# A mixture-of-experts layer whose gathers add expert results straight into the residual in SBUF

## The chip, the cores and the metric

The kernel runs on one core of a Trainium2 chip, in one launch. The metric is the device time of that launch in microseconds: the median of repeated runs.

## What is computed

The reference takes x of shape (16, 512, 128) in float32 and adds four sublayers to it, each on the layernorm of the running x: an attention without softmax (causal scores, 16 heads of 8 columns), a mixture of experts, an attention that keeps only its 6 strongest queries per head, and the same mixture of experts again. What matters here is the mixture:

```python
logits = xf @ router_w; probs = softmax(logits)       # 8192 tokens, 16 experts
w, idx = top_k(probs, 2)                               # two experts each
keep = rank_within_expert < capacity; w = where(keep, w, 0)
xe = x_pad[dispatch]                                   # rows sorted by expert
hidden = silu(xe @ gate_w[e]) * (xe @ up_w[e])
out = (hidden @ down_w[e]) * wbuf                      # scaled by its weight
combined.at[dispatch].add(out);  x = x + combined
```

## The kernel before

The tokens are 64 tiles of 128 tokens, 4 tiles to a batch, 16 batches. The residual x stays in SBUF all the time (`xs`, 128 x 64 x 128). The work goes through these stages, with all instruction streams written out by hand and tied by semaphores:

- First attention (`attention_a`, 16 batches). Beside it, a few batches behind, the router picks two experts for each token, and GpSimd (POOL) sends the normed rows to DRAM.
- First mixture, `experts(0)` and `experts(1)`: batches 0 to 7, then 8 to 15. Each has GRP = 24 groups of 512 rows.
- Second attention (`body`, called by `each_four`, 16 batches). For each batch b, the results of the first mixture for batch b+2 are fetched and added while the scores of b run.
- Second mixture, `experts(2)` and `experts(3)`, again 24 groups each; in `experts(3)` the fetching for batches 0 to 7 runs beside the groups. Then what is left of the fetching, and the output.

How rows move. `places` (L513) works out, on POOL, where each of a token's K = 2 copies goes, and the product of the router's weight and `keep`, which it leaves in `wts` in SBUF (L531). `send` (L498) issues 8 indirect scatters for a batch, tile by tile and both copies of a tile together: 128 rows of 512 bytes each from `xnf` to `dispA` or `dispB` in DRAM. `xnf` is a ring of NF = 3 buffers, and the norm of batch n waits until the sends of n-3 have landed. Before a mixture starts, its area's tails, and once the whole of `dispB`, are filled with zeros from `zeros`.

In `experts`, SyncE (SP) loads the rows of group g+4 (L387, two DMAs of 128 KB) when TensorE has turned group g (`xe_tp`), and then stores the results of group g-2 (L416). For each group TensorE turns the rows (`turn_x`, L1812), multiplies with the gate and up weights (L1823) and with the down weights of the group before (L1834); ScalarE evicts `xeT` (L845) and takes the silu (L850), VectorE (DVE) makes the hidden product (`hidden`, L1293), copies the result from PSUM to `ye` (`y_copy`, L1301), and then runs `pieces`, its share of other work. The order on DVE is hidden(g), y_copy(g-1), pieces(g).

Results come back by `fetch` (L557): for each batch, 8 indirect gathers on POOL, 128 rows each, from `ybufA` or `ybufB` into a buffer `yg` (shared with `vmyg`). `indices` on DVE copies the row numbers first (L1313), and a fetch waits for them. Then DVE adds each tile twice, xs = yg * wts + xs (L1318), eight instructions a batch: in groups 5 to 11 of `experts(1)` for the first two batches; in the scores of pairs 18 to 21 of each batch of the second attention; in groups 5 to 21 of `experts(3)`, where the indices of batch b+2 are made after the adds of batch b (`add_all`); and after it. The last batch is added in two parts (L1604), so that its first three tiles go out while the fourth is fetched. SP's `out` stores (L444 to L448) wait for the adds.

`stored(seg)` on POOL holds back the first fetch of a mixture half until all its results are in DRAM.

Of the kernel before, what the change touches and what calls it, by code (L numbers as in the profile page):

```python
# [5 lines left out]
F32 = mybir.dt.float32  # L6
# [7 lines left out]
P = 128  # L14
# [41 lines left out]
NF = 3  # L56


def build(nc, w, out):
    ctx = ExitStack()  # L60
    with ctx:
# [6 lines left out]
        def sem(name):  # L68
# [3 lines left out]
        dispA = nc.dram_tensor("dispA", [DUMMY + UR, D], F32).ap()  # L72
        dispB = nc.dram_tensor("dispB", [DUMMY + UR, D], F32).ap()
# [9 lines left out]
        wts = sb("wts", [P, NT * K])  # L83
# [21 lines left out]
        zeros = sb("zeros", [P, UT * D])  # L105
# [28 lines left out]
        xnf = [sb(f"xnf{r}", [P, TB, D]) for r in range(NF)]  # L134
# [22 lines left out]
        slg = [sb(f"slg{h}", [P, TB * K], I32) for h in range(2)]  # L157
        vmyg = sb("vmyg", [P, TB * GH * (D + DH)])
        vm = vmyg[:, :].rearrange("p (t x) -> p t x", t=TB)
        yg = [vmyg[:, h * TB * K * D:(h + 1) * TB * K * D].rearrange("p (j d) -> p j d", d=D) for h in range(2)]  # L160
# [29 lines left out]
        tails = sb("tails", [1, E], I32)  # L190

        apart = [sb(f"apart{h}", [P, GH, SEQ]) for h in range(2)]
        whose = sb("whose", [P, NT * K, E])
        xe = [[apart[h][:, r, :].rearrange("p (j d) -> p j d", d=D) for r in range(NX)] for h in range(2)]
# [43 lines left out]
                 "slg_ready got0 got1 got_end comb_head combined_head comb0 combined "  # L238
# [91 lines left out]
        def _(sp):  # L330
# [43 lines left out]
            for e in range(E):  # L374
# [3 lines left out]
                             zeros[:, :].unsqueeze(1).to_broadcast([P, SPAN // UR, UT * D])).then_inc(s["zeroed"], 16)  # L378
# [32 lines left out]
            def experts(seg):  # L411
# [29 lines left out]
            experts(3)  # L441
            for i in range(B - 1):
                sp.wait_ge(s["combined"], i + 1 + B)
                sp.dma_start(out_b[i], xs[:, tiles_of(i), :]).then_inc(s["x_out"], 16)  # L444
            sp.wait_ge(s["combined_head"], 1)
            sp.dma_start(out_b[B - 1][:, 0:TB - 1, :], xs[:, NT - TB:NT - 1, :]).then_inc(s["x_out"], 16)
            sp.wait_ge(s["combined"], 2 * B)
# [5 lines left out]
        def _(pool):  # L453
# [10 lines left out]
            pool.memset(vmyg[:, :], 0.0).then_inc(s["vm_zero"], 1)  # L464
# [33 lines left out]
            def send(g, i, h, tiles=range(TB)):  # L498

                if 0 in tiles:  # L500
                    pool.wait_ge(s["slots_ready"], g + 1)
# [1617 lines left out]
```

## Time and profile before

| | us |
|---|---|
| median of 3 runs | 1412.83 (1411.5 to 1418.56) |
| span of the profiled execution | 1555.5 |
| TensorE busy in the span | 1331.6 |
| VectorE busy | 1056.7 |
| GpSimd busy | 833.1 |
| ScalarE busy | 759.3 |

The profiled execution has no time of its own on record other than its span of 1555.5 us, from the first to the last instruction; it is 10% above the median of the runs without the profiler. All durations below are of that execution. The page gives the busy time of each engine, the span in slices, the DMA queues, the chain of work that ended last, and the costliest groups of instructions; the trace behind it can be asked for a stretch of time, an engine or a line.

### The profile page before, as it was taken

The page shows a single profiled execution, that of the slowest core. Times are in us where ns is not written, and L with a number is a line of the kernel's source. Part 1 is how long each engine was busy: PE and PEld are TensorE (multiplying, and loading weights), DVE is VectorE, ACT ScalarE, POOL GpSimd, SP SyncE. Part 2 cuts the span into 40 slices and gives each one's busy share as a digit, 9 for nine tenths or more (in the row PEclk, how much of TensorE's full clock was granted, in tenths as well). Part 3 has the DMA queues.
Part 4 walks back from the last instruction along what each step waited for, and adds up shares of the span by engine and source line. Part 5 has one row for each costly group of instructions (what it writes and reads, how often), then busy time and mean ns, then how long its engine had stood idle before and what let it go on. Part 6 is the DMA issues. An engine that isn't in the chain of part 4 may idle for free.

```text
span 1555.5 us, 28624 instructions
## 1 busy us (share of the span) xinstructions
PE 1331.6 (86%) x8534; PEld 822.4 (53%) x8534; DVE 1056.7 (68%) x4590; ACT 759.3 (49%) x1901; POOL 833.1 (54%) x1246
## 2 busy tenths in 40 slices
PE   3999998978996989999999999999999999767400
PEld 1566655547885955444444444444455588656400
DVE  2899998883643477888778788787798546433422
ACT  2444444424544666666556566555566455333200
POOL 3247776675323133466666567755555345435576
PEclk9999998987998988999889799887699899988755
DMA  6755312013444410000000000020001134444432
GB/s 171 244 171 188 115 38 69 25 52 111 157 151 135 137 31 15 15 21 28 25 25 28 18 25 28 27 77 23 23 18 42 34 122 153 132 129 138 145 79 73
DMA packets 119785, 125.82 MB, mean 81 GB/s; under 512 B 15568, under 2 KB 109904, under 8 KB 119632
## 3 DMA queue, kind: packets, MB, share of 16 engines
q1 hardware_dynamic: 103248, 90.42, 18.3%
q0 software_dynamic: 16384, 33.59, 7.5%
q8 instruction: 68, 1.11, 0.3%
q14 instruction: 85, 0.70, 0.2%
HBM read 50.15 MB, written 73.79 MB: 80 GB/s over the span
## 4 chain that ended last, share of the span: by engine, by line
PE 68%; DVE 9%; issue 6%; another core or an unknown queue 5%; POOL 5%; ACT 4%; DMA 0%; ACTq 0%; POOLq 0%; DVEq 0%
PE pair L1897 27%; PE pair L1823 8%; PE pair L1834 4%; POOL vmyg L563 4%; PE pair L1685 4%; PE bank L1709 3%; DVE pT L1126 2%; PE pair L1812 2%; PE bank L1630 2%; DVE pT L1401 2%; PE bank L1925 1%; PE bank L1624 1%; PE bank L1951 1%; PE pair L1674 1%
## 5 line engine op out<-in xcount | busy, mean ns | idle before, releaser
L1897 PE MATMUL pair<-kT,apart 32*128 32x512 f32 x2048 | 500.4, 733 | 8.0 <-DVE smax L1401 6.5
L1401 DVE CUSTOM_DVE_ANT_0 pT<-pair,pT 128x256 f32<-128x256 f32 x1024 | 385.4, 417 | 128.5 <-ACT pT L924 110.1
L924 ACT ACTIVATE pT<-pair 128x256 f32<-128x256 f32 x1024 | 327.1, 395 | 257.1 <-PE pair L1897 229.2
L1897 PEld LDWEIGHTS pair<-kT,apart 32*128 32x128 f32 x2048 | 198.5, 208 | 155.4 <-DVE smax L1401 97.8
L563 POOL DMA_INDIRECT vmyg<-ybufA,slg x128 | 123.2, 962 | 149.8 <-DVE smax L1401 67.3
L1293 DVE TENSOR_TENSOR hid<-sg,pair 128x512 f32<-128x512 f32 x96 | 65.9, 686 | 197.6 <-ACT sg L850 171.2
L1823 PE MATMUL pair<-xeT,unit_w 128*128 128x256 f32 x768 | 195.6, 400 | 0.8 <-issue 0.8
L563 POOL DMA_INDIRECT vmyg<-ybufB,slg x128 | 122.7, 958 | 91.9 <-DVE smax L1401 47.6
L1126 DVE TENSOR_TENSOR pT<-pair,causal 128x512 f32<-128x512 f32 x256 | 159.5, 681 | 12.5 <-PE pair L1685 12.3
L1834 PE MATMUL pair<-unit_w,hid 128*128 128x128 f32 x768 | 110.7, 291 | 61.9 <-DVE ye L1301 61.6
L508 POOL DMA_INDIRECT dispB<-xnf,sli x128 | 127.4, 996 | 63.7 <-issue 36.2
L1823 PEld LDWEIGHTS pair<-xeT,unit_w 128*128 128x128 f32 x768 | 149.0, 205 | 19.6 <-issue 1.2
L508 POOL DMA_INDIRECT dispA<-xnf,sli x128 | 128.3, 1002 | 56.5 <-issue 35.8
L1834 PEld LDWEIGHTS pair<-unit_w,hid 128*128 128x128 f32 x768 | 106.6, 204 | 72.6 <-DVE hid L1293 34.8
L1318 DVE SCALAR_TENSOR_TENSOR xs<-vmyg,wts,xs 128x128 f32<-128x128 f32 x248 | 80.1, 376 | 57.7 <-DMA vmyg<-ybufB,slg 54.6
L850 ACT ACTIVATE sg<-pair 128x512 f32<-128x512 f32 x96 | 57.3, 597 | 110.9 <-PE pair L1823 67.9
L857 ACT ACTIVATE unit_w<-f_w 128x384 f32 x160 | 74.9, 516 | 42.6 <-PE pair L1834 27.0
L1301 DVE COPY ye<-pair 128x512 f32<-128x512 f32 x96 | 65.8, 685 | 30.4 <-remote 17.8
L1401 DVE DVE_READ_ACCUMULATOR2_ANT smax<- 128x1 f32 x1024 | 83.1, 81 | 0.0
L550 POOL TENSOR_SCALAR lnv<-mv 128x4 f32<-128x4 f32 (+1 forms) x51 | 12.0, 235 | 132.8 <-DVE mv L1023 125.6
L845 ACT ACTIVATE xeT<-pair 128x512 f32<-128x512 f32 x96 | 56.3, 586 | 54.1 <-remote 26.6
L1685 PE MATMUL pair<-apart,kT 32*128 32x512 f32 x512 | 76.2, 665 | 7.6 <-DVE pT L1126 7.3
(231 smaller groups left out, 2008.0 us busy)
## 6 DMA issues: line engine op xcount, KB each, us to landing
dispB<-zeros SPq DMA_DIRECT2D x16, 1408.0 KB
apart<-dispA SPq DMA_DIRECT2D x96, 128.0 KB
ybufA<-ye SPq DMA_DIRECT2D x48, 256.0 KB
apart<-dispB SPq DMA_DIRECT2D x96, 128.0 KB
ybufB<-ye SPq DMA_DIRECT2D x48, 256.0 KB
dispA<-zeros SPq DMA_DIRECT2D x33, 128.0 KB
xs<-in_x SPq DMA_DIRECT2D x16, 256.0 KB, 3.2
out<-xs SPq DMA_DIRECT2D x15, 256.0 KB
```

What stands on the lines that cost most here:

```text
L508: pool.indirect_dma_start(out=area, out_offset=bass.IndirectOffsetOnAxis(ap=sli[h][:, K * j + k:K * j + k + 1], axis=0), in_=xnf[g % NF][: ...
L563: pool.indirect_dma_start(out=yg[h][:, j, :], out_offset=None, in_=ybuf[second(g)], in_offset=bass.IndirectOffsetOnAxis(ap=slg[h][:, j:j + ...
L857: last = act.activation(unit_w[g % NX][:, u, :], f_w[:, bass.ds(ex[u], 1), :].rearrange("p a n -> p (a n)"), ACT.Copy)
L924: act.activation(rel[n % RING][:, q, :], pair[n % RING][:, q, HALF:SEQ], ACT.Relu).then_inc(s["relu_done"], 1)
L1126: dve.tensor_tensor(pT[n % (2 * NG)][:, :, :], bank[4 + n % 4].rearrange("p (j t) -> p j t", j=GH), causal[:, :].unsqueeze(1).to_broadcast ...
L1293: dve.tensor_tensor(hid[h][:, :, :].rearrange("p j n -> p (j n)"), sg[h][:, :, :].rearrange("p j n -> p (j n)"), bank[4 + 2 * h][:, :], AL ...
L1318: last = dve.scalar_tensor_tensor(out=xb, in0=yg[h][:, K * j + k, :], scalar=wts[:, bass.ds((b * TB + j) * K + k, 1)], in1=xb, op0=ALU.mul ...
L1401: dve.tensor_tensor_reduce(out=rel[n % RING][:, q, :], in0=pair[n % RING][:, q, 0:HALF], in1=rel[n % RING][:, q, :], scale=1.0, scalar=LOW ...
L1685: pe.matmul(bank[4 + g][:, :].rearrange("p (j t) -> p j t", j=GH), kTs[h][at, c * P:(c + 1) * P], apart[h][at, :, c * P:(c + 1) * P], star ...
L1823: last = pe.matmul(bank[3 + 2 * h + k][:, u * UR:(u + 1) * UR], unit_w[r][:, u, k * D:(k + 1) * D], xeT[h][:, UT * u:UT * (u + 1), :].rear ...
L1834: last = pe.matmul(bank[7][:, j * D:(j + 1) * D], hid[h][:, j, :], unit_w[r][:, j // UT, 2 * D:3 * D], start=True, stop=True)
L1897: pe.matmul(pair[n % RING][:, q, :], apart[h][at, j, t * P:(t + 1) * P], kTs[h][at, HALF:], start=True, stop=True).then_inc(s["bsc_done"], 1)
```

## The change

The row of the dispatch area gets a 129th element, the token's weight for that expert. `xnf`, `zeros`, `dispA`, `dispB` and the `xe` buffers are widened from D = 128 to R = 129 elements. `places` writes the weight of the first choice into column 128 of `xnf` and keeps that of the second in `wsecond`. `send` no longer goes by tiles but by choices: first the four tiles with the first choice; then it waits until they have landed, POOL copies the second weight into the column, and the four tiles go out again. In `experts`, DVE copies the 4 weights of a group out of the loaded rows (`weights`, before `hidden`), and `y_copy` becomes a multiplication of PSUM by these weights. SP now stores group g-2 before it loads group g+4, and that load waits for `weights(g)` instead of the transposes. `fetch` gathers with the DMA's own addition straight into `xs`, four tiles of the first choice and four of the second, and the second choice waits for the first to have landed. The buffers `yg`, `slg` and `wts`, the index copies, and all additions on DVE are gone. In the tail the order is: batch b's first choice, then batch b-1's second.

```diff
+R = D + 1
-        dispA = nc.dram_tensor("dispA", [DUMMY + UR, D], F32).ap()
+        dispA = nc.dram_tensor("dispA", [DUMMY + UR, R], F32).ap()
...
             def load(seg, g):
                 if g >= NX:
-                    sp.wait_ge(s["xe_tp"], seg * GRP + g - NX + 1)
+                    sp.wait_ge(s["wrow_done"], seg * GRP + g - NX + 1)
...
                 for g in range(GRP - 1):
+                    if g >= 2:
+                        store(g - 2)
                     if g + NX < GRP:
                         load(seg, g + NX)
-                    if g >= 2:
-                        store(g - 2)
...
+            def send(g, i, h, parts=range(TB)):
                 area = disp[second(g)]
+                for part in parts:
+                    k = part // 2
+                    if part == 0:
+                        pool.wait_ge(s["slots_ready"], g + 1)
+                        pool.wait_ge(s["xw_done"], g + 1)
...
+                    if part == 2:
+                        pool.wait_ge(s[f"sent{h}"], 16 * TB * (K * i + 1))
+                        pool.tensor_copy(xnf[g % NF][:, :, D:R], wsecond[h][:, :, :]).then_inc(s["second_done"], 1)
+                        pool.wait_ge(s["second_done"], g + 1)
+                    for j in (part % 2 * 2, part % 2 * 2 + 1):
                         pool.indirect_dma_start(
...
-                pool.tensor_tensor(wts[:, cols].rearrange("p (t k) -> p t k", k=K), topw[:, :, :], keep[:, :, :], ALU.mult)
+                pool.tensor_tensor(wsecond[h][:, :, :], topw[:, :, 1:2], keep[:, :, 1:2], ALU.mult)
+                pool.tensor_tensor(xnf[g % NF][:, :, D:R], topw[:, :, 0:1], keep[:, :, 0:1], ALU.mult).then_inc(s["xw_done"], 1)
...
+            def fetch(b, g, k, tiles=range(TB), end=()):
+                h = g % 2
+                if 0 in tiles:
+                    pool.wait_ge(s["slots_made"], g // HALFB + 1)
+                    if g >= 2:
+                        pool.wait_ge(s[f"got{k}{h}"], g // 2 * 16 * TB)
+                    if k:
+                        pool.wait_ge(s[f"got0{h}"], (g // 2 + 1) * 16 * TB)
+                for t in tiles:
+                    at = (b * TB + t) * K + k
                     pool.indirect_dma_start(
-                        out=yg[h][:, j, :], out_offset=None, in_=ybuf[second(g)],
-                        in_offset=bass.IndirectOffsetOnAxis(ap=slg[h][:, j:j + 1], axis=0),
-                    ).then_inc(s["got_end" if j in end else f"got{h}"], 16)
+                        out=xs[:, b * TB + t, :], out_offset=None, in_=ybuf[second(g)],
+                        in_offset=bass.IndirectOffsetOnAxis(ap=slots[:, at:at + 1], axis=0), compute_op=ALU.add,
+                    ).then_inc(s["got_end" if t in end else f"got{k}{h}"], 16)
...
+                def weights(g):
+                    dve.wait_ge(s["xe_tp"], g + 1 + base)
+                    dve.tensor_copy(wrow[g % NX][:, :].unsqueeze(2), xe[seg % 2][g % NX][:, :, D:R]).then_inc(s["wrow_done"], 1)
...
-                    dve.tensor_copy(ye[h][:, :, :].rearrange("p j d -> p (j d)"), bank[7][:, :]).then_inc(s["y_ready"], 1)
+                    dve.tensor_tensor(ye[h][:, :, :], bank[7][:, :].rearrange("p (j d) -> p j d", d=D),
+                                      wrow[g % NX][:, :].unsqueeze(2).to_broadcast([P, GT, D]), ALU.mult).then_inc(s["y_ready"], 1)
...
-            def add_choice(b, h, k, done, tiles=range(TB)):
-                for j in tiles:
-                    last = dve.scalar_tensor_tensor(out=xb, in0=yg[h][:, K * j + k, :],
...
-                        add_first(b + 2, h, ((0, 1), (2, 3))[n - 18])
-                        add_second(b + 2, h, ((0, 1), (2, 3))[n - 20])
```

## Rows read from the trace of the kernel before

**Rows 1.** Busy time of each engine by stage (windows in us), as columns name.
```profile
core 0: us, PE busy (x) PEld busy (x) DVE busy (x) ACT busy (x) POOL busy (x), PEclk, DMA share, GB/s
352.00:461.00 109.00, 98.23 (x617) 88.98 (x618) 54.02 (x158) 55.91 (x106) 41.40 (x72) 0.90 0.44 140
461.00:549.00 88.00, 70.96 (x447) 64.05 (x447) 35.74 (x77) 45.28 (x90) 21.29 (x27) 0.92 0.44 136
549.00:1228.00 679.00, 668.98 (x3032) 323.23 (x3032) 544.29 (x2942) 413.34 (x1223) 395.02 (x544) 0.87 0.09 26
1228.00:1345.00 117.00, 101.56 (x614) 87.58 (x607) 60.65 (x217) 59.95 (x116) 46.51 (x76) 0.93 0.38 120
1345.00:1466.00 121.00, 85.11 (x465) 75.31 (x463) 48.61 (x109) 43.95 (x86) 59.74 (x63) 0.86 0.44 131
1466.00:1555.50 89.50, 0.00 (x0) 0.00 (x0) 23.77 (x89) 0.00 (x0) 62.43 (x66) 0.51 0.37 99
```

**Rows 2.** Timeline of POOL, gathers in experts(3) and behind it.
```profile
1348.26 1.01 POOL L563 DMA_INDIRECT vmyg<-ybufA,slg  x1 [4.51 <-DMA ybufA<-ye]
...
1469.32 0.94 POOL L563 DMA_INDIRECT vmyg<-ybufB,slg  x1 [1.28 <-issue]
...
1550.08 0.94 POOL L563 DMA_INDIRECT vmyg<-ybufB,slg  x1 [0.30 <-issue]
```

**Rows 3.** Waits: who waited for whom, us in total, times, longest.
```profile
POOL vmyg L563 <- DVE slg L1313: 48.6, 7, 13.3
```

**Rows 4.** SP timeline, then chain of waits, in clean groups of experts(1).
```profile
496.68 0.85 SPq L387 DMA_DIRECT2D apart<-dispB  x2
...
497.04 0.44 PE pair L1812 x4
497.48 1.73 PE pair L1823 x8
499.21 0.89 PE pair L1834 x8
```

**Rows 5.** Timeline of DVE, the last two adds of the kernel.
```profile
1552.73 0.74 DVE L1604 SCALAR_TENSOR_TENSOR xs<-vmyg,wts,xs 128x128 f32<-128x128 f32 x2 [0.84 <-DMA vmyg<-ybufB,slg]
```

**Rows 6.** Timeline of DVE in the second attention: a batch with adds, one without.
```profile
949.98 0.69 DVE L1439 TENSOR_REDUCE amax<-bank 128x1 f32<-128x512 f32 x1
961.95 0.27 DVE L1447 TENSOR_TENSOR cxm<-bank,block 128x128 f32<-128x128 f32 x1
...
1173.55 0.69 DVE L1439 TENSOR_REDUCE amax<-bank 128x1 f32<-128x512 f32 x1
1185.58 0.27 DVE L1447 TENSOR_TENSOR cxm<-bank,block 128x128 f32<-128x128 f32 x1
```

**Rows 7.** Timeline of DVE, two neighbouring groups of experts(1), adds between them.
```profile
491.31 0.68 DVE L1301 COPY ye<-pair 128x512 f32<-128x512 f32 x1
491.91 1.13 DVE L1318 SCALAR_TENSOR_TENSOR xs<-vmyg,wts,xs 128x128 f32<-128x128 f32 x4
...
494.37 0.68 DVE L1301 COPY ye<-pair 128x512 f32<-128x512 f32 x1
```

**Rows 8.** Groups of instructions: busy us, mean ns of one, idle before.
```profile
L508 POOL DMA_INDIRECT dispA<-xnf,sli x128 | 128.3, 1002 | 56.5 <-issue 35.8 <-DVE xs L1140 12.4 <-DVE pT L1126 4.9
L563 POOL DMA_INDIRECT vmyg<-ybufB,slg x128 | 122.7, 958 | 91.9 <-DVE smax L1401 47.6 <-issue 35.7 <-DVE slg L1313 8.6
L1293 DVE TENSOR_TENSOR hid<-sg,pair 128x512 f32<-128x512 f32 x96 | 65.9, 686 | 197.6 <-ACT sg L850 171.2 <-issue 24.9 <-DVE slots L1276 0.7
```

**Rows 9.** DMA queue of POOL: packets, MB, share of 16 engines.
```profile
q0 software_dynamic: 16384, 33.59, 7.5%
```

**Rows 10.** The last send of experts(2) (POOL), loads of experts(3) (SP), a scatter's landing (chain).
```profile
1323.56 0.97 POOL L508 DMA_INDIRECT dispB<-xnf,sli  x1 [0.30 <-issue]
1336.67 2.97 SPq L387 DMA_DIRECT2D apart<-dispB  x4
...
193.78 4.10 DMA dispA<-xnf,sli
```

More of the change, by code:

```diff
@@ L133, in build @@
         xnT = sb("xnT", [P, SEQ])
-        xnf = [sb(f"xnf{r}", [P, TB, D]) for r in range(NF)]
+        xnf = [sb(f"xnf{r}", [P, TB, R]) for r in range(NF)]
         xfT = sb("xfT", [P, SEQ])
@@ L156, in build @@
         sli = [sb(f"sli{h}", [P, TB * K], I32) for h in range(2)]
[L157 to L160, printed above, removed]
+        vm = sb("vm", [P, TB, GH * (D + DH)])
         cnt = sb("cnt", [P, K, E])
@@ L190, in build @@
         tails = sb("tails", [1, E], I32)
-        apart = [sb(f"apart{h}", [P, GH, SEQ]) for h in range(2)]
+        wsecond = [sb(f"wsecond{h}", [P, TB, 1]) for h in range(2)]
+        wrow = [sb(f"wrow{r}", [P, GT]) for r in range(NX)]
+        apart = [sb(f"apart{h}", [P, GH, GT * R]) for h in range(2)]
         whose = sb("whose", [P, NT * K, E])
-        xe = [[apart[h][:, r, :].rearrange("p (j d) -> p j d", d=D) for r in range(NX)] for h in range(2)]
+        xe = [[apart[h][:, r, :].rearrange("p (j d) -> p j d", d=R) for r in range(NX)] for h in range(2)]
         xeT = [sb(f"xeT{h}", [P, GT, D]) for h in range(2)]
@@ L656, in _ @@
             stored(0)
-            fetch(0, 0)
-            fetch(1, 1)
+            for k in range(K):
+                for b in range(2):
+                    fetch(b, b, k)
             def selected_rows(b):
@@ L754, in _ @@
             stored(2)
-            fetch(B, 0)
-            fetch(B + 1, 1)
-            for b in range(2, B):
+            for b in range(B):
                 if b == HALFB:
+                    fetch(b - 1, B + b - 1, 1)
                     stored(3)
-                fetch(B + b, b % 2, end=range(K * (TB - 1), K * TB) if b == B - 1 else ())
+                fetch(b, B + b, 0)
+                if b % HALFB:
+                    fetch(b - 1, B + b - 1, 1)
+            fetch(B - 1, 2 * B - 1, 1, end=(TB - 1,))
         @block.scalar
@@ L804, in keys_turns @@
                 for j in range(GH):
-                    last = act.activation(apart[h][:, j, :], qTs[h][:, :], ACT.Copy, scale=inturn[:, j:j + 1])
+                    last = act.activation(apart[h][:, j, 0:SEQ], qTs[h][:, :], ACT.Copy, scale=inturn[:, j:j + 1])
                 last.then_inc(s["turns_ready"], 1)
@@ L886, in masked_q @@
                 for j in turns:
[L887 removed]
+                    last = act.activation(apart[k][:, j, 0:SEQ], bank[0][:, :], ACT.Identity, bias=qbias[:, j:j + 1],
                                           scale=inturn[:, j:j + 1])
@@ L1466, in body @@
                         residual(b - 2)
-                    if fetch and n == 1:
-                        indices(b + 2, h)
                     if b == MID + 2 and n == 29:
```

123 lines of the change are left out of this document (31 added, 92 removed).

## The prediction

> **What bounds the kernel now.** I read the stages first [rows 1]. The reader is to see three kinds. In the second attention (679 us) TensorE is busy for 669; in the four halves of the mixture (109 + 88 + 117 + 121 = 435 us) no engine is full; in the last 89.5 us TensorE does nothing and POOL is busy for 62.4. That last stretch is a queue of gathers [rows 2]: the first gather of the second half starts at 1469.32, the 64th at 1550.08, 1.28 us apart on the average and 1.25 as a rule (0.94 of work, 0.30 between two). POOL issues them without a gap and nothing else decides. Ahead of it stand the 64 gathers of the first half, from 1348.26 on. They should take 64 x 1.25 = 80 us, but take 120, because POOL waited for index copies that DVE makes behind its adds: 48.6 us in 7 waits [rows 3], 8.6 of which lie in the second attention [rows 8] and 40.0 here. The gathers of the second half may start only when `experts(3)` has stored its last result, and the two came together: after 1469.32 less a wait of 1.28 [rows 2]. So in the profile the end of the kernel is: end of `experts(3)`, plus 64 gathers.
>
> Then the clean pace of a group [rows 4]: 0.44 for the transposes, 1.73 for gate and up, 0.89 for down, 3.06 us, all on TensorE. 96 groups at it are 294 us, and the four halves took 435: 141 us are stalls. The span of 1555.5 stands 142.7 above the median of 1412.83. That the two are so alike suggests that the timed runs have few of these stalls; it is an inference, and no row shows an execution without the profiler. It matters for the sum: undisturbed, `experts(3)` takes 24 x 3.06 = 73 us, less than the 80 us of its 64 gathers, so that in a timed run POOL's 128 gathers (160 us) follow each other from the end of `experts(2)` to the end of the kernel, in both kernels. I make the sum for the profiled execution and then say what the other picture changes.
>
> **What goes, with what it is worth.** (a) The 112 adds of the second attention, 8 a batch, and 14 index copies. A batch with adds and one without can be compared, both at the full clock (the granted level 2.4 GHz): from the reduction of `amax` to `cxm`, pairs 18 to 26, it is 949.98 to 961.95 = 11.97 us with the 8 adds and 4 statistics, and 1173.55 to 1185.58 = 12.03 without any of them [rows 6]. So these adds cost nothing: TensorE sets that stretch. The index copy stands where DVE is dense, at pair 1, at most 0.1 us a batch: 0 to -1.4 us; I take -1. (b) The adds of `experts(1)`: with four adds (1.13 us) between them two result copies are 3.06 apart [rows 7], the clean pace: 0. (c) The adds and index copies of `experts(3)`: 40 us of POOL's waits go, but the gathers they delay weren't late, since the end of the half came at the same time; in the undisturbed picture only the first of these waits stays, some 1.5 us (the index copy after group 6, at 7 x 3.06 = 21.4 us, against 20 us for 16 gathers). I take -1. (d) At the very end the two last adds, 0.74 us, and the step to them [rows 5]: -0.8.
>
> **What comes, and what hides it.** (e) `y_copy` as a multiplication reads PSUM and SBUF like `hidden`, which takes 686 ns [rows 8] where the copy took 0.68 [rows 7]: 0. The 96 weight copies of 4 numbers are 0.1 to 0.2 us each; DVE has room for 1.13 us more in a group at the clean pace [rows 7]: 0, and 96 x 0.15 = 14 us if that room were gone. (f) The load of group g+4 now waits for `weights(g)`, which stands behind y_copy(g-2) on DVE; so it goes out about one group (3.06 us) later than now. A load at 496.68 [rows 4] is for a group three clean groups on, some 9 to 10 us, of which 6 to 7 stay. The nearest row of a landing is 4.10 us, of a scatter [rows 10]: hidden, 0, and up to 1 us a group where the landing is over 7. (g) `send`: between the fourth and the fifth scatter POOL waits for landing, up to 4.10 less the 0.97 of issue, and copies a column (0.2). Beside the attentions these two are in different slots, tens of TensorE steps apart: 0. In a mixture they are back to back: +3.3 us for each of 3 batches. Behind the waiting POOL stands the next `places`, and for the last batch SP waits for its sends before it loads the first rows of the next half. Its last send starts at 1323.56, and SP loads at 1336.67 [rows 10]: 9 us of slack here after landing; at the clean pace the load would be due four groups after the sends began, about when they land. So 0 to 3.3 us at each of two places; I take +2 in all. (h) Rows of 516 bytes instead of 512 in the scatters, the loads and the zero fill, no longer at multiples of 512. No row shows such a transfer; DMA shares of 0.38 to 0.44 in the mixture [rows 1] leave room for a quarter more: 0, bounds 0 and +3. (i) The fetch of a second choice waits for the first. In the tail, four gathers of another batch (5.0 us) lie in between, which covers a landing of 4.10 with 0.9 to spare: 0. In the second attention POOL waits 1 to 3 us a batch, and it works 395 us of 679 [rows 1]: 0.
>
> (j) The price of a gather that adds. This decides, and no row shows one. The lower end is that of a gather now: 0.94 and 0.30. Nothing excludes less, but no reason speaks for it. For the upper end I take half as much again, as for three addresses a row (source, old value, target) instead of two: +0.47, which is 64 x 0.47 = 30 us behind `experts(3)`, and 128 x 0.47 = 60 if POOL has no gap in the timed runs. The nearest row between is the scatter, which differs from a gather in its direction and a bounds check: 1002 against 958 ns in the mean [rows 8], +0.04. One more operand should cost more than another direction, and less than half of everything, as a part of the 0.94 is fixed; I take +0.08, nearer to the scatter. In the profile's picture 64 x 0.08 = +5, in the undisturbed one 128 x 0.08 = +10. The transfers themselves stay hidden: the queue of POOL held 7.5% of 16 engines' 1555.5 us [rows 9], so each of 512 gathers and scatters took 0.075 x 1555.5 / 512 = 0.23 us of each engine; doubled, that is 0.46 in a cadence of 1.25.
>
> What the row shows here is a cost of issue, 0.94 us on POOL. The Trainium skill (Collectives: The Full Stack, the section on the bandwidth ceiling) says of an addition in the DMA engines that the add itself is free but needs two source reads, with two read descriptors on the same ring, and that such a transfer ran at about half the rate of a copy. By that rule the engines' 0.23 us would become up to 0.46, and the time would not change, since the issue sets the pace. If the second read descriptor also doubled POOL's whole work, the same 128 gathers would cost 128 x 0.94 = 120 us more; no row bears that out, and it is not in my sum. The skill's page DMA: Bandwidth & Descriptors calls the generation of descriptors a small, variable part of a DMA's fixed cost; by it, the surcharge would be near nothing.
>
> The sum: -1 -1 -0.8 +2 = -0.8 without the surcharge, and +10 for it in the picture that I hold likelier for timed runs: 1412.8 - 0.8 + 10 = 1422 us. In the profile's picture it is 1412.8 - 0.8 + 5 = 1417.
>
> **The rivals.** *No surcharge.* The adding gather is issued like any other. For it: 128 rows are few, and a scatter costs almost the same [rows 8]. Time: 1412.8 - 0.8 = 1412, between 1409 and 1415.
>
> *A dear gather.* From +0.25 to +0.47 on each, 128 times: +32 to +60, 1444 to 1472. For it: 0.94 us for 128 rows may well be work by the row. Against it: only that scatter and gather are so alike. The same side has a smaller case: if an adding gather lands later than the 5.0 us that lie between the two choices, each of 16 second fetches of the tail waits; at 7 us that is 16 x 2 = 32, 1444.
>
> *Faster.* `experts(3)` ends earlier, as its stalls are of the gathers' making. At the clean pace its 24 groups take 73 us, in the profile 121, 5.04 a group [rows 1]. In the changed kernel the first 64 gathers run without POOL's waits and are over by 1348 + 80 = 1428; the remaining 38 us to 1466 then hold 12 clean groups instead of 7.5, five groups less to do later: 5 x 3.06 = -15 us in the profile. It decides from the point where the stalls exist in timed runs and the surcharge is under 0.1 us: 1398 to 1405. Against it: the stalls are there in `experts(2)` too, which took 117 us with no gather beside it [rows 1]. One rule leads the same way: the Trainium skill (SBUF — State Buffer, the section on who interferes with whom) says that a DVE instruction with two inputs in SBUF, which an add is, holds back a GpSimd instruction that reads SBUF. The gathers beside adds and those without are equally long here, 0.94 [rows 2], so that I give it nothing.
>
> **How the numbers follow.** The forecast, a surcharge of 0.03 to 0.25, has 0.42: 1416 to 1444, with the likeliest at 1422. No surcharge 0.25. A dear gather 0.15, a late landing 0.05. Faster 0.13. For this kernel about 0.5%, 7 us, can be told from no change: 1405.8 to 1419.9. Faster by more: 0.13. Within: 0.25 and the 0.10 of the forecast that lies under 1420, 0.35. Slower: 0.32 + 0.15 + 0.05 = 0.52. The range from 1401 to 1450 leaves out half of the faster case and two thirds of the dear one, 0.17.
>
> **What would show it.** Right: the gathers of the tail on POOL have one length of 0.97 to 1.2 us, 0.30 apart, and still no gap; DVE loses some 34 us of busy time in the second attention (112 adds of 0.30) while that stage keeps its 679 us; the groups of `experts(1)` stay 3.06 apart; two columns' copies on POOL stand behind a wait of some 3 us in `experts(0)` and `experts(2)`. Wrong: gathers of 0.94 (then 1412); waits on the landing of the first choice in the tail; a TensorE that waits for loaded rows every group; or an `experts(3)` well under 121 us, which would make it faster.

## The result, and the profile after

The changed kernel takes 1562.85 us (median of 4 runs, 1556.42 to 1566.97) against 1412.38 beside it: 1.109 times as long [1.104, 1.114], 150 us more. The forecast was 1422, and the range ended at 1450.

The page of the changed kernel, parts 1 and 3:

```profile
span 1563.4 us, 28579 instructions
PE 1311.2 (84%) x8534; PEld 819.3 (52%) x8534; DVE 988.9 (63%) x4398; ACT 755.7 (48%) x1901; POOL 999.3 (64%) x1310
q0 software_dynamic: 45056, 33.72, 12.6%
```

VectorE has lost work, and POOL has 166 us more than in the first profile. The queue of POOL moves almost the same bytes as in [rows 9] (the scattered rows now have 516 bytes), in 45056 packets instead of 16384.

One thing has to be put right first. The profile of the kernel before stood 142.7 us above its median. The same kernel profiled again has a span of 1400.8 us, and it is this trace (`before_again`) that the changed one is laid beside. By stage (first mixture, second attention, second mixture, rest), the kernel before and then the changed one:

```profile
354.00:507.00 153.00, 149.54 (x979) 137.15 (x977) 86.88 (x228) 97.09 (x189) 58.14 (x84) 1.00 0.55 172
507.00:1143.00 636.00, 625.87 (x3098) 317.71 (x3099) 548.84 (x2993) 417.97 (x1237) 399.99 (x547) 0.95 0.10 30
1143.00:1302.00 159.00, 153.86 (x1016) 140.86 (x1014) 99.63 (x274) 97.14 (x188) 96.09 (x126) 1.00 0.58 177
1302.00:1401.00 99.00, 1.64 (x13) 1.29 (x11) 25.77 (x91) 0.25 (x1) 70.15 (x75) 0.52 0.36 100
```

```profile
360.00:515.00 155.00, 148.92 (x974) 136.70 (x972) 87.58 (x257) 96.85 (x189) 70.42 (x90) 1.00 0.60 170
515.00:1229.00 714.00, 692.19 (x3094) 348.96 (x3095) 516.60 (x2868) 417.36 (x1237) 470.64 (x573) 0.84 0.14 27
1229.00:1391.00 162.00, 157.28 (x1024) 144.10 (x1021) 92.40 (x266) 97.59 (x188) 102.06 (x115) 0.98 0.63 170
1391.00:1563.00 172.00, 1.20 (x9) 0.97 (x8) 1.83 (x3) 0.00 (x0) 140.94 (x92) 0.52 0.39 63
```

The columns are those of [rows 1]. The mixtures take almost the same. Two stages have grown: the end by 73 us, and the second attention by 78, in which TensorE's granted clock fell from 0.95 to 0.84. The end is the gathers; first, 65th and last of the second mixture on POOL, before and after:

```profile
1233.43 1.01 POOL L563 DMA_INDIRECT vmyg<-ybufA,slg  x1 [4.29 <-DMA ybufA<-ye]
1314.97 0.94 POOL L563 DMA_INDIRECT vmyg<-ybufB,slg  x1 [0.30 <-issue]
1395.59 0.94 POOL L563 DMA_INDIRECT vmyg<-ybufB,slg  x1 [0.30 <-issue]
```

```profile
1322.02 2.46 POOL L580 DMA_INDIRECT xs<-ybufA,slots  x1 [6.77 <-issue]
1441.43 1.55 POOL L580 DMA_INDIRECT xs<-ybufB,slots  x1 [0.30 <-issue]
1558.10 1.55 POOL L580 DMA_INDIRECT xs<-ybufB,slots  x1 [0.30 <-issue]
```

In both, 128 gathers follow each other from the end of `experts(2)` to the end of the kernel, 162.2 and 236.1 us from the start of the first to the start of the last. The work of one is 1.55 us instead of 0.94 [rows 2], the gap between two still 0.30: a surcharge of 0.60 us. (128 surcharges are 77 us, and the tail has grown by 74: in the 162.2 stand a gather of 1.99 us and a gap of 2.13, which `plain` below, with 158.6 us, doesn't have.)

Here is how the other stage loses time. TensorE in one batch of it, changed kernel (start, us, engine, line), and TensorE's windows around the place (columns as above, the clock third from the end):

```profile
793.51 1.13 PE L1855 MATMUL pair<-kT,apart 32*128 32x512 f32 x4
797.41 1.08 PE L1582 MATMUL bank<-ident,xnf 128*128 128x128 f32 x4 [2.77 <-POOL xnf L698]
798.42 2.08 PE L1855 MATMUL pair<-kT,apart 32*128 32x512 f32 x4
```

```profile
788.00:792.00 4.00, 4.00 (x19) 1.32 (x20) 3.43 (x17) 2.46 (x9) 3.63 (x3) 1.00 0.27 33
792.00:796.00 4.00, 2.64 (x16) 0.88 (x10) 3.13 (x19) 3.31 (x10) 3.68 (x6) 0.99 0.14 16
796.00:800.00 4.00, 2.59 (x8) 1.22 (x8) 0.32 (x2) 0.60 (x1) 3.42 (x5) 0.50 0.05 17
...
812.00:816.00 4.00, 4.00 (x14) 1.56 (x13) 3.18 (x25) 1.43 (x6) 1.34 (x2) 0.50 0.09 29
816.00:820.00 4.00, 3.92 (x24) 2.48 (x23) 3.15 (x15) 2.52 (x9) 0.93 (x2) 0.95 0.08 25
```

TensorE stands for 2.77 us, since POOL hasn't finished the normed rows `xnf` that the router needs. Behind it the granted clock is 0.50 (the 1.2 GHz level) for some 20 us, although TensorE is busy without a break again from 797.41 on, and the same four score matmuls take 2.08 us instead of 1.13. In the kernel before, `xnf` is ready (838.43 + 1.04, a row shown further down) about 4.1 us before TensorE asks:

```profile
843.62 0.66 PE L1624 MATMUL bank<-ident,xnf 128*128 128x128 f32 x4
```

The stage windows say how much of the loss is clock. What the granted share falls short of full is 0.05 x 636 = 32 us in the kernel before and 0.16 x 714 = 114 us in the changed one: 82 us more, where the stage grew by 78, and TensorE is busy for 692 of its 714 us. So nearly all of this stage's loss is time that TensorE worked at the lower level; the waits themselves are short.

### The profile page after: what moved, and what is told of

Read it like the earlier page. It is cut to its first block and busy times, and to the rows that moved or that the text cites. A ratio compares the mean times of both kernels' runs of the same rounds, so it can differ in the third digit from the quotient of the medians.

```text
span 1563.4 us, 28579 instructions
## 1 busy us (share of the span) xinstructions
PE 1311.2 (84%) x8534; PEld 819.3 (52%) x8534; DVE 988.9 (63%) x4398; ACT 755.7 (48%) x1901; POOL 999.3 (64%) x1310
## 3 DMA queue, kind: packets, MB, share of 16 engines
q0 software_dynamic: 45056, 33.72, 12.6%
## 5 line engine op out<-in xcount | busy, mean ns | idle before, releaser
L580 POOL DMA_INDIRECT xs<-ybufA,slots x128 | 200.1, 1563 | 110.7 <-DVE smax L1403 67.5
L580 POOL DMA_INDIRECT xs<-ybufB,slots x128 | 199.8, 1561 | 85.9 <-DVE smax L1403 51.4
L1781 PE MATMUL pair<-xeT,unit_w 128*128 128x256 f32 x768 | 185.4, 385 | 0.0
L1146 DVE TENSOR_TENSOR pT<-pair,causal 128x512 f32<-128x512 f32 x256 | 159.5, 681 | 14.8 <-PE pair L1643 14.5
L1781 PEld LDWEIGHTS pair<-xeT,unit_w 128*128 128x128 f32 x768 | 141.2, 194 | 15.4
L1792 PE MATMUL pair<-unit_w,hid 128*128 128x128 f32 x768 | 101.9, 276 | 8.9 <-DVE ye L1327 8.9
L1792 PEld LDWEIGHTS pair<-unit_w,hid 128*128 128x128 f32 x768 | 100.1, 192 | 15.7 <-DVE hid L1313 10.7
L1327 DVE TENSOR_TENSOR ye<-pair,wrow 128x512 f32<-128x512 f32 x96 | 65.7, 684 | 11.4 <-issue 7.3
L1667 PE MATMUL bank<-pT,vm 128*32 128x128 f32 x2048 | 71.5, 282 | 0.0
L1770 PE MATMUL pair<-ident,apart 128*128 128x128 f32 x384 | 60.6, 282 | 6.0 <-ACT xeT L865 3.2
```

The lines of the kernel that those rows point to most:

```text
L580: pool.indirect_dma_start(out=xs[:, b * TB + t, :], out_offset=None, in_=ybuf[second(g)], in_offset=bass.IndirectOffsetOnAxis(ap=slots[:, ...
L1146: dve.tensor_tensor(pT[n % (2 * NG)][:, :, :], bank[4 + n % 4].rearrange("p (j t) -> p j t", j=GH), causal[:, :].unsqueeze(1).to_broadcast ...
L1667: last = pe.matmul(bank[1][at:at + QG, c * P:(c + 1) * P], vm[:, c, j * P + at:j * P + at + QG], pT[c % 2 * NG + g][:, j, :], start=(c == ...
L1781: last = pe.matmul(bank[3 + 2 * h + k][:, u * UR:(u + 1) * UR], unit_w[r][:, u, k * D:(k + 1) * D], xeT[h][:, UT * u:UT * (u + 1), :].rear ...
L1792: last = pe.matmul(bank[7][:, j * D:(j + 1) * D], hid[h][:, j, :], unit_w[r][:, j // UT, 2 * D:3 * D], start=True, stop=True)
```

## The experiments

Where gathers don't add, they replace the rows of the residual, which is lost; such kernels serve for their time alone. Beside the kernels, the one before ran at 1407.51, 1408.08, 1406.64, 1409.2 and 1402.9 in the five groups of runs.

**Which profile is typical.** `before_again`: the kernel before, unchanged.

> The kernel before, once more with a profile, to see whether the span of its first profile (1555.5 us, against a median of 1412.8) belongs to every profiled execution. If the 141 us of stalls in the mixture halves belong to that one execution, this profile has a span near 1413, the four halves last about 4 x 74 to 80 = 300 us, and POOL's 128 gathers follow each other from the end of experts(2) to the end. If they belong to the profiler, the span is again near 1555 and the halves near 435 us.

1402.55 us, span 1400.8. The 48 groups of each mixture last 153 and 159 us, 312 where the first profile had 435: most of the stalls belonged to the first profile's execution, and the "undisturbed picture" of the prediction is the right one.

**The addition or the rest.** `plain` has no `compute_op`; the edit of `add_first` is below, and `add_second` has `g >= B` in its place:

```diff
                         in_offset=bass.IndirectOffsetOnAxis(ap=slots[:, at:at + 1], axis=0),
-                        compute_op=ALU.add,
+                        **({"compute_op": ALU.add} if g < B else {}),
```

> The changed kernel with the DMA's addition left out of all gathers: a gathered row replaces the one in xs, so that the residual is lost. All else stays: carried weights, scaled results, split sends, order of loads and stores. Theory A (the addition in the gathers makes the whole loss, in the tail and in the second attention): gathers of 0.94 us, 0.30 apart, and a time within 10 us of before, 1405 to 1422. Theory B (the addition costs only its surcharge of 0.60 on the 128 gathers of the tail, 77 us, and the other edits make the remaining 73): 1486, from 1475 to 1497.

> The changed kernel with the DMA's addition only in the gathers of the first mixture (beside the second attention); those of the second mixture replace the residual. Theory A: 1563 - 128 x 0.60 = 1486, since the tail is freed of its surcharge, and the loss of 73 in the second attention stays. Theory B: 1486 too, as the 73 belong to the other edits. The second attention lasts about 715 us, and the tail about 160 for 128 gathers. This run checks the 77; the two theories are told apart by the next one.

> The changed kernel with the DMA's addition only in the gathers of the second mixture; those of the first replace the residual. Theory A (adding gathers cost 73 in the second attention): 1413 + 77 = 1490, from 1480 to 1500, and a second attention near 640 to 650 us. Theory B (they cost nothing there): 1563, from 1555 to 1570, and a second attention near 715.

`plain` 1404.53, 0.9985 [0.995, 1.002] of the kernel before; `add_first` 1491.37 (1.058); `add_second` 1480.15 (1.052). Theory A holds. Carried weights, scaled results, split sends, wider rows, the order of loads and stores, and all of VectorE's additions are together worth nothing. The additions cost 76 us in the second mixture and 87 in the first; the sum, 162, is close to the 158 between `plain` and the changed kernel. In `add_second` the second attention has its old length, and the tail shows the surcharge alone:

```profile
1245.20 1.64 POOL L580 DMA_INDIRECT xs<-ybufA,slots  x1 [7.01 <-issue]
1363.89 1.55 POOL L580 DMA_INDIRECT xs<-ybufB,slots  x1 [0.30 <-issue]
1480.61 1.55 POOL L580 DMA_INDIRECT xs<-ybufB,slots  x1 [0.31 <-issue]
```

**Is it the addition by itself?** `before_adding`: the kernel before, with the addition in its gathers (on top of what stands in `yg`).

```diff
-                        in_offset=bass.IndirectOffsetOnAxis(ap=slg[h][:, j:j + 1], axis=0),
+                        in_offset=bass.IndirectOffsetOnAxis(ap=slg[h][:, j:j + 1], axis=0), compute_op=ALU.add,
```

> The kernel before with the DMA's addition in its gathers (into yg, on top of what stands there) and nothing else changed; DVE still adds. If the addition in the gathers is the whole loss, whatever else is changed: 1407 + 77 + 75 = 1559 (1540 to 1575), gathers of 1.55 us. If it needs the other edits (the wait of a second choice for the first, the split sends): at most 1407 + 77 = 1484 with a second attention of 640.

1507.11 (1.071). Neither of the two forecasts: the tail is 74 us longer as it should be, but the second attention lasts 663 us, not 715. So the surcharge costs some 25 us there in the old order, and the change brings something that triples it.

**Lateness or transfers?** `half` (only second choices add), `ahead` (the fetches earlier in the batch), `late_plain` and `late_more` (nothing adds, but POOL has extra copies to make).

```diff
                 if fetch_:
-                    pair_made(1)
-                    fetch(b + 2, b + 2, 0, (0, 1))
+                    fetch(b + 2, b + 2, 0)
                 if b >= 3:
                     places(b - 3, b - 3 + B, 1 - h)
...
+                    fetch(b + 2, b + 2, 1)
```

```diff
                     ).then_inc(s["got_end" if t in end else f"got{k}{h}"], 16)
+                    if g < B:
...
+                        pool.tensor_copy(linger[n % 4][:, :], zeros[:, 0:240]).then_inc(s["lingered"], 1)
```

> The changed kernel with the DMA's addition only in the gathers of the second choices; those of the first choices replace the residual. POOL is then late by 4 x 0.60 = 2.4 us a batch instead of 4.8. Theory A (a threshold: in the kernel before the normed rows are ready at 839.5 where TensorE asks for them at 843.6, so that up to 4.1 us of lateness cost nothing): second attention 637 to 645 us, the tail 64 x 0.60 = 38 us longer, 1405 + 38 = 1443 (1435 to 1452). Theory B (every adding gather costs its share, wherever it stands): 1405 + (75 + 77) / 2 = 1481, second attention near 678.

> The changed kernel, complete, with the gathers of the second attention issued earlier in each batch: all four of the first choice before places, all four of the second right behind it, without their waits for score pairs. Theory A (the dearer gathers make POOL late with the normed rows xnf; TensorE waits for them 1 to 3 us a batch, and its granted clock falls to 0.50 for some 16 to 20 us afterwards; together 75 us): the norm is done 4 to 5 us earlier, TensorE no longer waits for it, the second attention lasts 637 to 645 us, and the time is 1563 - 75 = 1488 (1478 to 1498). Theory B (the adding transfers themselves disturb the attention, whenever they are issued, or POOL's work as a whole is the bound): the second attention stays above 700 and the time at 1555 to 1570.

> The kernel `plain` (gathers replace the residual, none adds), with one more copy on POOL (128 x 240 elements, some 0.6 us by the nearest row, 0.73 for 128 x 256) behind each gather of the second attention, so that POOL is as late as with adding gathers but no DMA adds. Theory A (POOL's time alone makes the loss): the second attention lasts 700 to 730 us and the time is 1405 + 75 = 1480 (1460 to 1495), with TensorE waiting for xnf. Theory B (the adding transfers make it): second attention 640, time 1405 (1400 to 1415).

> As late_plain, but two copies of 0.39 us behind each gather of the second attention instead of one, since in late_plain the spacing of the gathers rose only from 1.25 to 1.53 us. Still no gather adds. The spacing should be 1.9 us here, as with adding gathers (1.85), and POOL 8 x 0.65 = 5.2 us late a batch. Theory A (POOL's time alone makes the loss of the second attention): TensorE waits 1 to 3 us a batch for xnf, the stage lasts 700 to 735 us, the time is 1405 + 60 to 95, 1465 to 1500. Theory B (it takes the adding transfers too): 660 us as in late_plain and 1420 at most.

`half` 1453.31: 49 over `plain`, of which the tail's 64 adding gathers are 39.6. At most 9 are left for the second attention, not 38, and in the trace the stage lasts 640 us as in `plain`. `ahead` 1500.61: the stage is back at 645 us. `late_plain` 1415.74: my copies were only 0.39 us, and the spacing 1.53. `late_more` 1463.38: with two copies the gathers stand 1.85 us apart, just as adding ones do, and without a single addition the stage lasts 688 us and the time rises by 59. So POOL's time alone makes at least two thirds of the 87 us that `add_first` loses, more than theory B allowed and a little less than theory A wanted. The other 28 us aren't told apart: the adding transfers may have a part in them, but in `late_more` POOL also waited less for the first choice to land (1.56 us in a typical batch instead of 2.40), since two copies cover part of that wait. What TensorE waited for the normed rows in the second attention (us in total, times, longest), in the changed kernel, `half`, `ahead`, `late_more`:

```profile
PE bank L1582 <- POOL xnf L698: 13.8, 11, 2.8
```

```profile
PE bank L1582 <- POOL xnf L698: 4.5, 7, 0.9
```

```profile
PE bank L1576 <- POOL xnf L698: 1.5, 2, 1.3
```

```profile
PE bank L1592 <- POOL xnf L708: 16.4, 10, 3.6
```

**What triples it.** My next reading was a plain sum: 4.1 us of slack, less 4.8 for eight surcharges, less 1.0 for the copy of the second weight. `no_copy` takes the copy and its waits away.

```diff
-                    if part == 2:
-                        pool.wait_ge(s[f"sent{h}"], 16 * TB * (K * i + 1))
-                        pool.tensor_copy(xnf[g % NF][:, :, D:R], wsecond[h][:, :, :]).then_inc(s["second_done"], 1)
-                        pool.wait_ge(s["second_done"], g + 1)
```

> The changed kernel, with all gathers adding, but without the copy of the second weight in send and the two waits around it (rows of the second choice then carry the first choice's weight). It gives POOL back 0.19 + 0.81 = 1.0 us a batch in the second attention. In the kernel before the normed rows have 4.1 us of slack, in `plain` 3.1. Theory A (a threshold: slack less 4.8 us of dearer gathers is -0.7 without the copy, as in before_adding, against -1.7 with it): the second attention falls from 715 to about 663 us, and the time from 1563 to 1511 (1500 to 1525): 16 us of POOL's work are worth some 50. Rival (each microsecond of POOL's work costs one): 1563 - 16 = 1547.

1555.08, 8 us less, and not clear of the noise: 1.106 [1.100, 1.113] against 1.109 [1.104, 1.114]. The 52 us of theory A are excluded; the rival's 16 lie at the edge of what the noise allows. The 1.0 us lies ahead of a place where POOL is idle for 3 us anyway, until the next batch's first score pair. Another of the change's waits does stand in the way. POOL at the fifth gather of a batch, the first of a second choice, in the kernel before and in `plain`:

```profile
829.00 0.94 POOL L563 DMA_INDIRECT vmyg<-ybufB,slg  x1 [0.30 <-DVE smax L1401]
```

```profile
827.70 0.96 POOL L580 DMA_INDIRECT xs<-ybufB,slots  x1 [0.31 <-issue]
831.07 0.94 POOL L580 DMA_INDIRECT xs<-ybufB,slots  x1 [2.42 <-DVE smax L1403]
```

The trace puts the 2.42 us down to DVE, but DVE had long been done; the other semaphore of this wait is the landing of the first choice. 827.70 + 0.96 + 2.42 = 831.08, and a gather lands 2.6 us after issue here. In `aside` below, which has the same wait for DVE and none for landing, the gap is 0.30 in every batch. The order within `xs` costs 2.1 us more than the old gap in each batch. `aside` takes it away (second choices of the first mixture add into a buffer of their own), and `pe_later` leaves POOL as it is and lets TensorE ask two pairs later; `both` is `ahead` and `pe_later` together.

```diff
-                    if k:
+                    if k and g >= B:
                         pool.wait_ge(s[f"got0{h}"], (g // 2 + 1) * 16 * TB)
...
-                        out=xs[:, b * TB + t, :], out_offset=None, in_=ybuf[second(g)],
+                        out=aside[h][:, t, :] if k and g < B else xs[:, b * TB + t, :], out_offset=None, in_=ybuf[second(g)],
```

```diff
-                    if before and n == 23:
+                    if before and n == 25:
                         turn(b - 2 + B, "ffn", xnf[(b - 2 + B) % NF])
...
-                    if before and n == 25:
+                    if before and n == 27:
                         logits(b - 2 + B, bank[0])
```

> The changed kernel, all gathers adding, but in the second attention those of the second choice add into a buffer of their own, so that they need not wait for the first choice to land (the second choice's results are left out of the residual there). The tail is as in the changed kernel. Theory (lateness adds up against a slack): the normed rows have 4.1 us of slack in the kernel before; the changed kernel takes 8 x 0.60 = 4.8 us for the surcharge and 2.1 us for the wait for landing (2.40 of idle in place of 0.30), 2.8 us too much; without the wait it is 4.8 - 4.1 = 0.7 too much, as in before_adding. Second attention near 663 us, time 1563 - 52 = 1511 (1500 to 1525). Rival (the wait for landing hides in POOL's other waits, and costs nothing): 1563, stage 700 to 715.

> The changed kernel, complete; only the order around the router in the second attention is moved: TensorE turns the normed rows at score pair 25 instead of 23, the logits, their exponentials and DVE's routing steps follow two pairs later. POOL does exactly the same. Theory A (what costs is that TensorE stands waiting for xnf, and the clock that it loses by it): the slack grows by two pairs, 2.4 us, against a lack of 2.8; TensorE waits 0.4 us or less, the granted clock of the stage is back at 0.93 or more, the second attention lasts 640 to 655 us and the time is 1563 - 75 to 60, 1488 to 1503. Theory B (POOL's amount of work, or the adding transfers, sets the stage's length): 1555 to 1570.

> ahead and pe_later together, a complete kernel. If the second attention is at its floor with a slack of 2 us or more, it lasts 638 to 642 us and only the tail's surcharge is left: 1405 + 128 x 0.60 = 1482 (1475 to 1490). It shows what the change costs at its best order; if it stays at 1495 to 1500 as ahead, something else of 15 us is left in the change.

`aside` 1508.9, as its theory had it: with dear gathers, the wait for landing is worth 54 us; in `plain`, which has it too, it costs nothing. `both` 1497.25 [1.055, 1.074]: the stage has 642 us, and the time over `plain` is the tail's 77 plus 16 (its runs lie between 1487.5 and 1509.5). But `pe_later` 1528.93 gave back 34 us, not 60 to 75. The stage in `plain`, `both`, `aside` and `late_more` (columns of [rows 1]):

```profile
514.00:1154.00 640.00, 632.20 (x3101) 320.83 (x3102) 513.98 (x2868) 418.91 (x1238) 401.92 (x573) 0.94 0.10 30
519.00:1161.00 642.00, 626.73 (x3104) 322.11 (x3105) 520.86 (x2870) 417.81 (x1238) 459.05 (x565) 0.94 0.15 29
521.00:1179.00 658.00, 645.02 (x3104) 327.87 (x3105) 519.05 (x2869) 418.77 (x1238) 470.88 (x573) 0.92 0.15 29
515.00:1203.00 688.00, 658.85 (x3101) 333.56 (x3102) 521.80 (x2869) 418.68 (x1238) 485.40 (x797) 0.90 0.10 28
```

Taking off each time what the clock falls short of full (length times 1 less the granted share) leaves 602, 604, 605 and 619 us, against 604 in the kernel before and 600 in the changed one. The stage is long where the clock is low, and for little else (15 us in `late_more`).

What was still open is why TensorE waited at all in `pe_later`. I read POOL's queue batch by batch, and ran `pe_later` once more for its trace.

> pe_later once more, since it gave back only 34 of the 75 us that theory A wanted (1529 instead of 1488 to 1503), for a trace of it. New reading of the traces so far: POOL's own queue is the bound. Its work and issue gaps are 33.8 us a batch in the kernel before, against a period of 38.3 that TensorE sets; in the kernels with adding gathers they are 39 to 40, more than 38.3. Where the fetches are not pinned (ahead, both, aside, before_adding) the period is 40 and the stage 642 to 663. Where they wait for score pairs and for landings, that idle time comes on top: here 2.5 to 4 us, since POOL does the same as in the changed kernel. By it this trace shows batches of 42 to 43 us, a stage of 675 to 695 us, and a time near 1529 (1515 to 1540). If the loss were TensorE's waiting and clock alone, the stage would be 640 to 655.

1525.13. The end of the norm in successive batches (POOL), in the kernel before, in `both` and in `pe_later_again`:

```profile
838.43 1.04 POOL L680 TENSOR_TENSOR xnf<-xnf,nmr 128x512 f32<-128x512 f32 x1
...
876.72 1.04 POOL L680 TENSOR_TENSOR xnf<-xnf,nmr 128x512 f32<-128x512 f32 x1
```

```profile
810.88 1.04 POOL L698 TENSOR_TENSOR xnf<-xnf,nmr 128x512 f32<-128x512 f32 x1
...
851.05 1.04 POOL L698 TENSOR_TENSOR xnf<-xnf,nmr 128x512 f32<-128x512 f32 x1
```

```profile
823.13 1.04 POOL L698 TENSOR_TENSOR xnf<-xnf,nmr 128x512 f32<-128x512 f32 x1
...
865.25 1.04 POOL L698 TENSOR_TENSOR xnf<-xnf,nmr 128x512 f32<-128x512 f32 x1
```

Periods of 38.3, 40.2 and 42.1 us. I took POOL's idle times of over 0.31 us from each, but for the 0.81 us that it waits for its own copy of the second weight. Before, the rest (work and issue gaps) is 33.8 us, and TensorE's 38.3 set the pace. With adding gathers the rest is 39 to 40 in every kernel, more than 38.3: POOL is the bound of such a batch even where it hardly waits (`both`: 0.5 us of waits). Over the whole stage that costs little, 642 us in `both` against 640 in `plain`, since there some batches take 40 to 47 us in any case. In `pe_later_again` 2.5 to 4 us of pinned waits (for landings, and for the score pairs that a fetch is tied to) come on top, and the period is 42 to 43; the stage has 670 us, a little under what I expected. In the changed kernel the waits are 4 to 10 us, since TensorE, standing and then slowed, makes the score pairs late for which POOL's fetches wait.

**What the surcharge goes by.** `shape`, `shape_plain`: the second mixture's gathers fetch 64 rows (first half) or rows of 256 bytes (second half), with and without addition.

```diff
-                        out=xs[:, b * TB + t, :], out_offset=None, in_=ybuf[second(g)],
+                        out=xs[0:half, b * TB + t, 0:wide], out_offset=None,
+                        in_=ybuf[second(g)].rearrange("r (a d) -> (r a) d", d=wide),
...
```

> The changed kernel, but in the second mixture the adding gathers fetch less: for batches 0 to 7 only 64 rows of 512 bytes, for batches 8 to 15 all 128 rows but of 256 bytes (the rest isn't fetched). If POOL's work goes by rows: 128 rows of 256 bytes still take 1.55 us, and 64 rows take about half of the variable part, 0.9 to 1.2 us. If it goes by bytes, both take the same, 0.9 to 1.2. If it is fixed by the instruction, both stay at 1.55.

> As shape, but the gathers of the second mixture don't add (they replace). With shape it gives the fixed part and the part by row of a plain gather. If the 0.94 us are mostly fixed, 64 rows take 0.8 or more; if mostly by row, 0.5 to 0.6. The surcharge of an adding gather by row is then 0.60 / 128 = 4.7 ns if it grows with the rows.

Groups of both, adding first (128 rows of 256 bytes, then 64 rows of 512; busy us, mean ns):

```profile
L582 POOL DMA_INDIRECT xs<-ybufB,slots x64 | 99.1, 1548 | 19.5 <-issue 19.5
L582 POOL DMA_INDIRECT xs<-ybufA,slots x58 | 82.3, 1418 | 17.7 <-issue 17.4 <-DMA xs<-ybufA,slots 0.3
```

```profile
L582 POOL DMA_INDIRECT xs<-ybufB,slots x64 | 60.4, 944 | 19.5 <-issue 17.7 <-DMA xs<-ybufB,slots 1.8
L582 POOL DMA_INDIRECT xs<-ybufA,slots x58 | 52.2, 899 | 17.7 <-issue 17.4 <-DMA xs<-ybufA,slots 0.3
```

Half the bytes change nothing (1548 and 944 ns), half the rows little: 1418 and 899. The surcharge is 0.60 us with 128 rows and 0.52 with 64: nearly all of it belongs to the instruction. One run of each stands behind this, with some 60 gathers to a group.

## Why the prediction was wrong

- **The frame** was right: `before_again` shows that most of the profile's 141 us of stalls were not in the timed runs (the halves take 312 us instead of 435), and that 128 gathers stand in a row behind `experts(2)`. The main number was rightly made for that picture. That 141 and 142.7 were so alike was in part luck: the halves are 123 us shorter, the second attention is 43 shorter too (636 instead of 679, at a clock of 0.95 instead of 0.87), and the end some 10 longer.
- **(a) to (d), what goes.** DVE lost 32 us of busy time in the second attention (549 to 517), and nothing was gained by it. With `plain` at 0.9985 of before, the sum of -0.8 us for everything but the addition is borne out as a sum; it says nothing of each term. One is known: no gather in the tail of `before_again` waited for an index copy (0.30 us between two), so that (c) had nothing to give.
- **(b)** hid one small miss: from TensorE's first turn to its last down product the first mixture takes 162.0 to 166.6 us where the first gathers add, and 159.5 to 161.2 in `before_again`, `plain`, `add_second` and `late_plain`. In the changed kernel DVE waits once for 4.5 us for gathers of the first batch.
- **(e), (f), (h)** cost nothing that `plain` could show. **(g)** the wait in `send` is there beside the mixture, 2.0 to 3.6 us, and takes no time from the end.
- **(i) failed for the second attention.** I set the wait for the first choice at 0, because "POOL waits 1 to 3 us a batch, and it works 395 us of 679". That is an average over the stage, it leaves out the 0.30 us between two issues, and the idle time lies in other places. The wait lies on the way to the norm that TensorE needs: 2.1 us a batch, and 54 us in all once the gathers add (`aside`), most of it by the clock that TensorE loses behind its waits, for which the sum had no term. In the tail, where (i) was put at 0 as well, the gathers keep their 0.30.
- **(j) failed by its size and by its place.** Size: 0.60 us, over the upper bound of 0.47, which came from a picture of three addresses instead of two; a fixed cost of the instruction was not in that picture. 128 x 0.60 = 77 us of the 150. Place: I counted the surcharge only in the tail. The first mixture's 128 gathers add too: 16 beside `experts(1)`, and 112 in the second attention, 4.8 us a batch, where POOL's queue had 4.5 us to spare in 38.3.
- **The rivals.** "A dear gather" named the mechanism and the 128 times; its price was 32 to 60. A late landing didn't come in the tail: an adding gather lands 3.3 us after issue, and four gathers of another batch now take 7.4. The transfers became dearer, as the prediction allowed. An adding gather makes (45056 - 16384) / 256 = 112 packets more than a plain one. Part 2 of the profile's page counts 32768 more of them under 2 KB and 4096 fewer between 2 and 8 KB, which is 128 packets of one row each in place of 16 of eight rows. In `plain` the queue's share was 8.6% of 1409.6 us, 0.237 us for each of its 512 transfers; in the changed kernel it is 12.6% of 1563.4 us = 197, and less 256 x 0.237 for the scatters that leaves 0.53 for each adding gather, 2.2 times as much. The Trainium skill (Collectives: The Full Stack, the bandwidth ceiling) says that an add in the DMA engines takes two source reads and two read descriptors and runs at about half the rate. The 2.2 times agree with that rate; whether they come of a second read or of the many small packets, no run here tells. POOL's own work rose by 0.64 of itself, not by the whole; by doubling, the tail would have cost 120. The Trainium skill's page DMA: Bandwidth & Descriptors (Anatomy of one DMA) calls descriptor generation small and variable. That led to no surcharge, and the measured 0.60 us decide against it.
- **The parts together.** Of the 158 us between `plain` and the changed kernel, 77 are the tail. The other 81 are almost all the second attention (714 us instead of 640), and there nearly all is the lower clock: it falls short of full by 114 us against 38 in `plain`. POOL's queue over TensorE's pace, without pinned waits, is worth 2 to 5 us of the stage (`both` 642, `ahead` 645). The times of these two lie 16 and 19 us over `plain` plus the tail's 77; 4 to 5 us of that are the first mixture, and the rest isn't placed. What isn't told apart either is how much clock a wait costs: 13.8 us of TensorE's waits for `xnf` go with a clock of 0.84 in the changed kernel, 16.4 us with 0.90 in `late_more`.

No kernel here beats the one before. The best complete one with adding gathers is `both`, 88 us behind it.

## What to carry to other kernels

Work taken off an engine with room (VectorE) is worth nothing, and a little work put on the engine that issues transfers can be dear: count an issuing engine's time with the gaps between its issues, batch by batch, against the period of the engine that sets the pace. Count a new cost in every stage where the instruction occurs, and for each wait ask who needs the next thing in that queue, and by when; a mean share of idle time answers neither. Where TensorE is the pace, a wait of 1 to 3 us can cost several times its length, since the clock may fall behind it: here 13.8 us of waits went with 78 us of stage. Multiply the length of a stage by what its granted clock falls short of full before you look for other causes.

## What the runs showed of the hardware

- An indirect gather of 128 rows of 512 bytes that adds takes 1.55 us on GpSimd against 0.94 for one that doesn't (changed kernel, `before_again`), lands 3.3 us after issue against 2.5, and makes 144 packets instead of 32 (the latter by 16384 / 512): each row goes as a packet of its own, where a plain gather moves eight rows in one.
- This cost hardly depends on what is fetched: halving the rows takes 0.13 us off the adding gather and 0.05 off the plain one, halving the bytes of a row nothing (`shape`, `shape_plain`).
- Two gathers behind each other are 0.30 us apart; with a small POOL instruction between, the gap ahead of the second is 0.17 (`late_more`: 0.16 behind the copies).
- A TensorE wait of 2.77 us was followed by some 20 us at the lower clock level, 0.50, although TensorE was busy again all that time.
